# A local-attention block between two FFN layers on one core: four 64x64 tiles for the scores, values four units behind, x turned in the seventh unit

## Chip, cores and metric

The kernel runs on one core of one Trainium2 chip. The time is device microseconds of a whole execution. A comparison of this kernel can tell about 0.3% from no change.

## What is computed

The input is 4 batches of 2048 tokens of 256 numbers (float32). Three layers follow one another, each added to x:

```
x = x + 0.5 * ffn(layernorm(x));  x = x + attention(layernorm(x));  x = x + 0.5 * ffn(layernorm(x))
attention, 16 heads of 64, blocks of 128 tokens:
  q = x Wq / 8; k = x Wk; v = x Wv
  side_k, side_v: Wk, Wv on the sums of 16 tokens (128 per batch)
  logits of a block: q against the keys of the block left of it, itself, the block right of it
    (masked to |distance| <= 127 and to the batch), and against the 128 side keys
  probs = softmax with one extra logit of 0;  y = probs v;  out = y Wo
```

Only the attention phase is changed. Of the left block a query in row i sees keys i+1 and up, and of the right block keys up to i-1.

## The kernel before

**Precision.** Operands are kept as two float16 parts, high and low, and each product is three matmuls (high by high, high by low, low by high). So each stage writes a high part (ScalarE, `high`, L1263, or `split_high`, L1302) and then a low part (VectorE, `low`, L1346; for the probabilities GpSimd, `split_low`, L1013).

**Units.** The 64 blocks of 128 tokens are done in 16 rounds of `RING` = 4 blocks, and a block in 16 units, one for each head. Every engine has its program written out unit by unit, and each runs its own list in order. For head v:

- TensorE makes its scores (`scores`, L1122 and L1125) four to seven units ahead. It does four heads at once, as two pairs, in units 0, 4, 8 and 12 of a block. A pair is an even head in partitions 0 to 63 and an odd head in 64 to 127, each a matmul of 64 rows by 128 columns (a 64x128 tile) into its own PSUM bank. Key tiles whose ring slots are neighbours are one matmul.
- VectorE adds the mask and takes the maximum four units ahead (`largest`, L1354), ScalarE takes the exponential three ahead (L1286), the high parts are made two ahead (L1302, for every fourth head VectorE, L1366), then the low parts on GpSimd.
- SyncE issues one DMA transpose of both parts one unit ahead (L987), into one of `NPARTS` = 6 buffers.
- TensorE does its 12 matmuls of values `PV_LAG` = 3 units behind (`values`, L1147), so in unit u those of head u - 3. They wait for the landed transpose (`turned`).

**Items.** Between scores and values TensorE works through the projections of neighbouring blocks in pieces, as `PIECES` lists them by unit: V1 and V0, Q0, Q1, K0, K1, the output projection OUTP in four pieces, and three turns by matmuls with the identity: XTR (normalised x of a later block), YT1 and YT0 (the two halves of y). What a unit finishes, ScalarE and VectorE take out of PSUM at their next unit (`due`): ScalarE first thing in its unit, VectorE first thing in units 0, 4, 8, 12 and after `largest` in the others. XTR and YT1 use the same bank (`y_ps[1]`). XTR waits for `normalise_y` of the earlier block's second half, YT1 for XTR's low part, and OUTP's third piece (unit 10) for YT1's low part:

```
def project_out(bank, turned_y, pieces=(0, 1, 2, 3)):
    if 2 in pieces:
        pe.wait_ge(lo_done, turned_y + 1)
```

**Keys** are stored as `[slot, part, head pair, token]`, a ring of four blocks and a fifth slot with the side keys. The order of the four key tiles changes with the block's place in its round, so that slots stand next to each other where they can.

Of the kernel before, what the change touches and what calls it, by code (L numbers as in the profile page):

```python
# [6 lines left out]
F16 = mybir.dt.float16  # L7
# [8 lines left out]
P = 128  # L16
# [4 lines left out]
H, DH = 16, 64  # L21
# [13 lines left out]
FRONT, BEHIND = 1, 3  # L35
# [6 lines left out]
class Persistent:  # L42
# [24 lines left out]
    def block(self, n):  # L67

        if isinstance(n, int):
            return self.x[:, FRONT + n, :]  # L70
        return self.x[:, bass.ds(n + FRONT, 1), :].rearrange("p a d -> p (a d)")
# [626 lines left out]
def attention_phase(nc, w):  # L698
# [23 lines left out]
    V1, Q0, XTR, Q1, YT1, K0, OUTP, K1, YT0, V0 = PLAIN = range(10)  # L722
    SK0, SK1, SV0, SV1 = range(10, 14)
    FIRST_ORDER = [SK1, V1, Q0, XTR, Q1, SV1, YT1, K0, OUTP, K1, YT0, V0]
    LAST_ORDER = [V1, Q0, XTR, Q1, YT1, K0, SK0, OUTP, K1, YT0, V0, SV0]
# [5 lines left out]
    PIECES = [[(V1, 0)], [(V1, 1)], [(Q0, 0)], [(Q0, 1)], [(XTR, 0), (Q1, 0)], [(Q1, 1)], [(OUTP, 0)], [(OUTP, 1), (YT1, 0)],  # L731
              [(K0, 0)], [(K0, 1)], [(OUTP, 2)], [(OUTP, 3)], [(K1, 0)], [(K1, 1)],
              [(YT0, 0), (V0, 0)], [(V0, 1)]]
    XTR_SLOT = 4
# [12 lines left out]
    SCORE_AHEAD, EXP_AHEAD, SPLIT_AHEAD, TURN_AHEAD, PV_LAG = 4, 3, 2, 1, 3  # L747
    NBUF = 4
    NPARTS = 6
# [9 lines left out]
    with ExitStack() as ctx:  # L759
# [17 lines left out]
        kr = sb("k_parts", [P, RING + 1, 2, HD], F16)  # L777
# [45 lines left out]
        y_cleared = sem("y_cleared")  # L823
# [127 lines left out]
        def tiles_of(at, v):  # L951
# [4 lines left out]
            return tiles if place == INNER else tiles[1:]  # L956

# [90 lines left out]
        def _(pe):  # L1048
# [53 lines left out]
            def scores(at, v):  # L1102
# [9 lines left out]
                cols = slice(pair * P, (pair + 1) * P)  # L1112
                todo, started = tiles_of(at, v), False
                while todo:

                    (t, slot), n = todo[0], 1
                    while n < len(todo) and todo[n][1] == slot + n:
                        n += 1
                    todo = todo[n:]
                    for q_part, k_part in ((HI, HI), (HI, LO), (LO, HI)):  # L1120
                        ends = not todo and q_part == LO
                        even = nc.tensor.matmul(score_ps[v % NBUF][:, t * P:(t + n) * P],  # L1122
                                                qs[0:DH, j % 2, q_part, cols], kr[0:DH, slot:slot + n, k_part, cols],
                                                start=not started, stop=ends, skip_group_check=True)
# [59 lines left out]
            for index, (kind, n) in enumerate(PRE):  # L1184
                if index == FIRST_SCORES:
                    pe.wait_ge(lo_done, FIRST_SCORES)
                    for v in range(0, SCORE_AHEAD, 2):
                        scores(At(0, 0), v)
# [311 lines left out]
```

## Time and profile before

| | |
|---|---|
| median of 3 runs | 2176.99 us (2176.89 to 2182.71) |
| profiled execution, its own time | 2183.18 us |
| its span | 2181.5 us |
| attention phase in it | 310 to 1928 us, 1618 us |
| FFN phases | 0 to 310 us, 1928 to 2181 us |
| busy share of the whole span: TensorE, VectorE, ScalarE, GpSimd | 94%, 86%, 88%, 64% |
| mean granted TensorE clock, share of 2.4 GHz | 0.991 |

The busy share of an engine is the time in which at least one of its instructions runs. For TensorE matmuls (PE) and weight loads (PEld) are told apart; matmuls are pipelined, so that a matmul's duration is longer than the distance from its start to the next start. That distance is what it costs in a stream.

### The profile page before, as it was taken

Reading aid. Unit: us, or ns where it says so; the run is one execution under the profiler, and the core shown is the slowest. Engines: PE = TensorE matmul, PEld = TensorE weight load, DVE = VectorE, ACT = ScalarE, POOL = GpSimd, SP = SyncE. Lnnn points to the kernel's source line nnn. Section 1 sums busy time; section 2 is a strip of 40 time slices with the busy share of each in tenths; the row PEclk is TensorE's granted clock in tenths of the full one; section 3 lists DMA queues with packets and bytes.
Section 4 is the critical chain, followed back from the end, with each engine's and each line's share of the span. In section 5 each row is a group of like instructions: output and inputs, shape, how many; then the busy total and the mean of one; then the engine's idle time right before and its main releaser. Section 6 shows DMA issues by size and latency. Waiting matters only on the chain. (4 is left out here: it accounts for less than half of the span.)

```text
span 2181.5 us, 77479 instructions
## 1 busy us (share of the span) xinstructions
PE 2049.6 (94%) x30286; PEld 1567.5 (72%) x30286; DVE 1879.6 (86%) x4646; ACT 1930.1 (88%) x4210; POOL 1406.1 (64%) x1455
## 2 busy tenths in 40 slices
PE   5999979999999999999999999999999999979999
PEld 3666657777777777777777778777777777746666
DVE  7999968889998898898979899998889889867776
ACT  5899958999999899999989999998999999969997
POOL 2444536777787687777767777786777777722221
PEclk9999989999999999999999999999999999989999
DMA  7888837999999899999989999999999999958998
GB/s 210 154 156 153 158 61 124 172 166 176 171 173 171 132 174 170 172 178 168 171 143 162 172 174 169 178 179 152 149 171 172 169 177 175 163 87 177 179 179 182
DMA packets 1341581, 355.54 MB, mean 163 GB/s; under 512 B 1321760, under 2 KB 1340192, under 8 KB 1341216
## 3 DMA queue, kind: packets, MB, share of 16 engines
q1 hardware_dynamic: 1341216, 350.59, 100.4%
q8 instruction: 239, 3.92, 0.7%
q14 instruction: 126, 1.03, 0.2%
HBM read 14.68 MB, written 8.39 MB: 11 GB/s over the span
## 5 line engine op out<-in xcount | busy, mean ns | idle before, releaser
L1013 POOL TENSOR_TENSOR probs_split<-probs,probs_split 128x512 f16<-128x512 f32 (+1 forms) x1026 | 1159.3, 1130 | 385.3 <-ACT probs_split L1302 281.3
L1286 ACT ACTIVATE probs<-probs,minus_max 128x512 f32<-128x512 f32 (+1 forms) x1027 | 717.0, 698 | 27.1 <-DVE minus_max L1354 26.9
L1354 DVE CUSTOM_DVE_ANT_0 probs<-score_ps,mask,neg_qk_scale 128x512 f32<-128x512 f32 (+1 forms) x1028 | 723.5, 716 | 9.6 <-PE score_ps L1125 8.3
L1147 PEld LDWEIGHTS y_ps<-v_parts,probsT 128*128 128x128 f16 x11904 | 457.7, 98 | 149.4 <-DMA probsT<-probs_split 71.1
L1147 PE MATMUL y_ps<-v_parts,probsT 128*128 128x64 f16 x11904 | 514.8, 193 | 51.4 <-DMA probsT<-probs_split 49.8
L1302 ACT ACTIVATE probs_split<-probs 128x512 f16<-128x512 f32 (+1 forms) x770 | 470.2, 611 | 8.5 <-DMA probsT<-probs_split 0.3
L1122 PE MATMUL score_ps<-k_parts,q_parts 64*128 64x384 f16 (+3 forms) x2604 | 371.1, 286 | 4.7 <-DVE k_parts L1346 2.7
L1125 PE MATMUL score_ps<-k_parts,q_parts 64*128 64x384 f16 (+3 forms) x2604 | 371.1, 286 | 0.0
L1122 PEld LDWEIGHTS score_ps<-k_parts,q_parts 64*128 64x128 f16 x2604 | 200.5, 94 | 108.0 <-issue 13.2
L1054 PE MATMUL item_ps<-b_xT,wk_split 128*128 128x128 f16 x3168 | 221.7, 220 | 1.9 <-DVE v_parts L1346 1.5
L1054 PE MATMUL item_ps<-wo_split,yT_parts 128*128 128x256 f16 x1560 | 213.9, 274 | 6.1 <-DVE v_parts L1346 4.6
L1054 PE MATMUL item_ps<-b_xT,wq_split 128*128 128x128 f16 x3120 | 218.2, 220 | 1.2 <-DVE b_xT L1346 0.9
L1054 PE MATMUL item_ps<-wv_split,b_xT 128*128 128x512 f16 x786 | 212.3, 380 | 0.0
L1054 PEld LDWEIGHTS item_ps<-b_xT,wk_split 128*128 128x128 f16 x3168 | 180.3, 98 | 35.7 <-issue 22.1
L1366 DVE CAST probs_split<-probs 128x512 f16<-128x512 f32 (+1 forms) x256 | 181.0, 707 | 27.8 <-ACT probs L1286 27.7
L1125 PEld LDWEIGHTS score_ps<-k_parts,q_parts 64*128 64x128 f16 x2604 | 200.4, 94 | 0.0
L1286 ACT ACTIVATION_READ_ACCUMULATOR probs<-probs,minus_max 128x1 f32 x1027 | 194.2, 189 | 0.0
L1054 PEld LDWEIGHTS item_ps<-b_xT,wq_split 128*128 128x128 f16 x3120 | 178.6, 98 | 18.7 <-issue 12.9
L1054 PEld LDWEIGHTS item_ps<-wo_split,yT_parts 128*128 128x128 f16 x1560 | 135.7, 98 | 19.5 <-DVE v_parts L1346 5.1
L1346 DVE TENSOR_TENSOR yT_parts<-y_ps,yT_parts 128x512 f16<-128x512 f32 x129 | 88.5, 686 | 54.4 <-ACT yT_parts L1263 54.3
L1346 DVE TENSOR_TENSOR v_parts<-item_ps,v_parts 128x512 f16<-128x512 f32 x140 | 95.7, 686 | 43.5 <-ACT v_parts L1263 43.4
L1263 ACT ACTIVATE k_parts<-item_ps 128x512 f16<-128x512 f32 x141 | 84.2, 597 | 53.8 <-PE item_ps L1054 51.5
(172 smaller groups left out, 3452.1 us busy)
## 6 DMA issues: line engine op xcount, KB each, us to landing
probsT<-probs_split SPq DMA_TRANSPOSE x1025, 3.9
out_x<-x_resident SPq DMA_DIRECT2D x64, 128.0 KB, 2.0
x_resident<-in_L_attn_x SPq DMA_DIRECT2D x56, 128.0 KB, 2.7
h_a<-in_L_ffn_w_up SPq DMA_DIRECT2D x1, 1024.0 KB, 5.8
scratch_a<-in_L_ffn_w_down SPq DMA_DIRECT2D x1, 1024.0 KB, 8.0
x_resident<-in_L_attn_x SPq DMA_DIRECT2D x2, 512.0 KB, 9.4
raw_q_a<-in_L_attn_Wq SPq DMA_DIRECT2D x1, 1024.0 KB, 11.5
raw_k_a<-in_L_attn_Wk SPq DMA_DIRECT2D x1, 1024.0 KB, 11.8
```

The source lines that it names most:

```text
L1013: nc.gpsimd.tensor_tensor(parts_of[ring(at, v)][:, LO, low_columns(place_of(at, v))], probs[v % NBUF][:, cols], parts_of[ring(at, v)][:, H ...
L1054: last = nc.tensor.matmul(out, left(k, a), right(k, b), start=(k == 0 and m == 0), stop=(k == n - 1 and m == 2))
L1122: even = nc.tensor.matmul(score_ps[v % NBUF][:, t * P:(t + n) * P], qs[0:DH, j % 2, q_part, cols], kr[0:DH, slot:slot + n, k_part, cols], ...
L1125: odd = nc.tensor.matmul(score_ps[v % NBUF + 1][:, t * P:(t + n) * P], qs[DH:P, j % 2, q_part, cols], kr[DH:P, slot:slot + n, k_part, cols ...
L1147: last = nc.tensor.matmul(out, pt[ring(at, v)][:, low * a + t, :], vr[:, slot, b, h * DH:(h + 1) * DH], start=(n == 0), stop=(n == len(pas ...
L1263: nc.scalar.activation(dst, src, ACT.Copy).then_inc(hi_done, 1)
L1286: nc.scalar.activation(probs[v % NBUF][:, cols], probs[v % NBUF][:, cols], ACT.Exp, bias=bias[:, j % 2, h:h + 1], scale=-1.0, accum_out=su ...
L1302: nc.scalar.activation(parts_of[ring(at, v)][:, HI, cols], probs[v % NBUF][:, cols], ACT.Copy).then_inc(phi_done[v % 4], 1)
L1346: nc.vector.tensor_tensor(dst, src, hi, ALU.subtract).then_inc(lo_done, 1)
L1354: nc.vector.tensor_tensor_reduce(out=probs[v % NBUF][:, cols], in0=score_ps[v % NBUF][:, cols], in1=mask_of(at, v), scale=w.neg_qk_scale[: ...
L1366: nc.vector.tensor_copy(parts_of[ring(at, v)][:, HI, cols], probs[v % NBUF][:, cols]).then_inc(phi_done[v % 4], 1)
```

## The change

- `scores`: the 64x128 tiles become 64x64 tiles, four at a time: two halves of the queries (`side` 0 and 1) by two heads. The half of the right block's keys that queries 0 to 63 can't see is left out for them, and the half of the left block's keys that queries 64 to 127 can't see. A new function `key_runs` gives the runs of neighbouring keys for each side. The parts are now the outer loop, the runs the inner one.
- The keys' layout becomes `[part, head pair, slot and token]`.
- The four score banks are cleared on VectorE once at the phase's start, and TensorE waits for this once.
- `PV_LAG` 3 to 4, `NPARTS` 6 to 7. `invert_denominators` and `normalise_y` move one unit later.
- XTR moves from unit 4 (after Q1's piece) to unit 6 (before OUTP's), YT1 from unit 7 to 8. OUTP's third piece stays in unit 10.
- Two of three spare blocks behind the resident x are dropped, and `block` clips its index.

```diff
-FRONT, BEHIND = 1, 3
+FRONT, BEHIND = 1, 1
...
-    V1, Q0, XTR, Q1, YT1, K0, OUTP, K1, YT0, V0 = PLAIN = range(10)
+    V1, Q0, Q1, XTR, YT1, K0, OUTP, K1, YT0, V0 = PLAIN = range(10)
...
-    PIECES = [[(V1, 0)], [(V1, 1)], [(Q0, 0)], [(Q0, 1)], [(XTR, 0), (Q1, 0)], [(Q1, 1)], [(OUTP, 0)], [(OUTP, 1), (YT1, 0)],
-              [(K0, 0)], [(K0, 1)], [(OUTP, 2)], [(OUTP, 3)], [(K1, 0)], [(K1, 1)],
+    PIECES = [[(V1, 0)], [(V1, 1)], [(Q0, 0)], [(Q0, 1)], [(Q1, 0)], [(Q1, 1)], [(XTR, 0), (OUTP, 0)], [(OUTP, 1)],
+              [(K0, 0), (YT1, 0)], [(K0, 1)], [(OUTP, 2)], [(OUTP, 3)], [(K1, 0)], [(K1, 1)],
               [(YT0, 0), (V0, 0)], [(V0, 1)]]
-    XTR_SLOT = 4
+    XTR_SLOT = 6
...
-    SCORE_AHEAD, EXP_AHEAD, SPLIT_AHEAD, TURN_AHEAD, PV_LAG = 4, 3, 2, 1, 3
+    SCORE_AHEAD, EXP_AHEAD, SPLIT_AHEAD, TURN_AHEAD, PV_LAG = 4, 3, 2, 1, 4
     NBUF = 4
-    NPARTS = 6
+    NPARTS = 7
     CLEARED = 4
...
-        kr = sb("k_parts", [P, RING + 1, 2, HD], F16)
+        kr = sb("k_parts", [P, 2, NPAIR, (RING + 1) * P], F16)
...
+        def key_runs(at, v, side):
+
+            order, runs = order_of(at, v), []
+            for t, slot in tiles_of(at, v):
+                first = DH if order[t] == LEFT and side == 1 else 0
+                end = DH if order[t] == RIGHT and side == 0 else P
+                to, source, n = t * P + first, slot * P + first, end - first
+                if runs and runs[-1][0] + runs[-1][2] == to and runs[-1][1] + runs[-1][2] == source:
+                    runs[-1][2] += n
+                else:
+                    runs.append([to, source, n])
+            return runs
...
-                cols = slice(pair * P, (pair + 1) * P)
-                todo, started = tiles_of(at, v), False
-                while todo:
-
-                    (t, slot), n = todo[0], 1
-                    while n < len(todo) and todo[n][1] == slot + n:
-                        n += 1
-                    todo = todo[n:]
-                    for q_part, k_part in ((HI, HI), (HI, LO), (LO, HI)):
-                        ends = not todo and q_part == LO
-                        even = nc.tensor.matmul(score_ps[v % NBUF][:, t * P:(t + n) * P],
-                                                qs[0:DH, j % 2, q_part, cols], kr[0:DH, slot:slot + n, k_part, cols],
-                                                start=not started, stop=ends, skip_group_check=True)
-                        odd = nc.tensor.matmul(score_ps[v % NBUF + 1][:, t * P:(t + n) * P],
-                                               qs[DH:P, j % 2, q_part, cols], kr[DH:P, slot:slot + n, k_part, cols],
-                                               start=not started, stop=ends, skip_group_check=True)
-                        started = True
+                runs = [key_runs(at, v, side) for side in range(2)]
+                last = {}
+                for q_part, k_part in ((HI, HI), (HI, LO), (LO, HI)):
+                    for run in range(max(map(len, runs))):
+                        for side in range(2):
+                            if run >= len(runs[side]):
+                                continue
+                            queries = slice(pair * P + side * DH, pair * P + (side + 1) * DH)
+                            to, source, n = runs[side][run]
+                            ends = q_part == LO and run == len(runs[side]) - 1
+                            for odd in range(2):
+                                rows = slice(odd * DH, (odd + 1) * DH)
+                                last[odd] = nc.tensor.matmul(
+                                    score_ps[v % NBUF + odd][side * DH:(side + 1) * DH, to:to + n],
+                                    qs[rows, j % 2, q_part, queries], kr[rows, k_part, pair, source:source + n],
+                                    start=(run == 0 and q_part == k_part), stop=ends, skip_group_check=True)
+                even, odd = last[0], last[1]
...
+                    pe.wait_ge(scores_cleared, NBUF)
...
+                    if h == XTR_SLOT:
+                        block_item(at, b, j, XTR, (0,))
                     for kind, piece in PIECES[h]:
                         if kind not in TURNS:
                             block_item(at, b, j, kind, (piece,))
-                    if h == XTR_SLOT:
-                        block_item(at, b, j, XTR, (0,))
...
+            values(end, -4)
...
-                return kr[:, slot, part, 512 * c:512 * c + 512]
+                return kr[:, part, 4 * c:4 * c + 4, slot * P:(slot + 1) * P]
...
+            for n in range(NBUF):
+                nc.vector.memset(score_ps[n][:], 0.0).then_inc(scores_cleared, 1)
...
-                    if h in (2, 10):
-                        invert_denominators(at, u - 3)
                     if h in (3, 11):
-                        normalise_y(at, u - 4, at.before(j) if h == 3 else at.item(j, YT1) + 1)
+                        invert_denominators(at, u - 4)
+                    if h in (4, 12):
+                        normalise_y(at, u - 5, at.before(j) if h == 4 else at.item(j, YT1) + 1)
                     for n, kind in due_late(at, u):
```

## Rows read from the trace of the kernel before

**Rows 1.** Windows: span's phases; per engine busy us (instructions), clock, DMA share.
```profile
310.00:1928.00 1618.00, 1549.03 (x26662) 1226.64 (x26662) 1417.30 (x3505) 1465.42 (x3559) 1215.97 (x1221) 1.00 1.08 164
...
500.00:1700.00 1200.00, 1154.87 (x20011) 915.28 (x20008) 1062.36 (x2629) 1101.02 (x2679) 918.50 (x922) 1.00 1.10 167
```

**Rows 2.** Groups by form, 500 to 1700 us, VectorE: out<-in xcount | busy, mean ns | idle.
```profile
L1402 DVE RECIPROCAL inv_denominator<-denominator 128x8 f32<-128x8 f32 x97 | 18.1, 187 | 0.0
```

**Rows 3.** Waits of the attention phase: engine, for what: us, times, longest.
```profile
PEld y_ps L1147 <- DMA probsT<-probs_split: 71.1, 124, 1.7
...
ACT k_parts L1263 <- PE item_ps L1054: 51.5, 104, 2.6
...
PEld item_ps L1054 <- issue: 45.5, 144, 0.4
...
ACT yT_parts L1263 <- PE y_ps L1087: 32.2, 51, 2.4
...
ACT b_xT L1263 <- PE y_ps L1080: 16.8, 18, 6.8
...
DVE probs L1354 <- PE score_ps L1125: 8.3, 16, 1.1
...
PEld score_ps L1122 <- DVE minus_max L1354: 6.5, 27, 0.5
...
PEld item_ps L1054 <- DVE yT_parts L1346: 5.2, 10, 1.7
```

**Rows 4.** Timeline of TensorE's matmuls: start, us, line, out<-in, count [idle before].
```profile
993.18 0.83 PE L1054 MATMUL item_ps<-b_xT,wk_split 128*128 128x128 f16 x12
...
994.20 0.82 PE L1054 MATMUL item_ps<-wo_split,yT_parts 128*128 128x256 f16 x6
...
998.75 0.83 PE L1054 MATMUL item_ps<-b_xT,wk_split 128*128 128x128 f16 x12
1000.14 0.52 PE L1147 MATMUL y_ps<-v_parts,probsT 128*128 128x64 f16 x12 [0.56 <-DMA probsT<-probs_split]
```

**Rows 5.** The DMA transposes: durations of issue, and to landing.
```profile
L987 SPq DMA_TRANSPOSE probsT<-probs_split x1025: 1209/1287/2722, 327.3 to 1917.4; - x171
...
DMA to landing us min/median/max: 2.7/3.9/6.0
```

**Rows 6.** Waits of the DMA queue, 500 to 1700 us.
```profile
SPq L987 <- POOL probs_split L1013: 564.7, 621, 2.6
```

**Rows 7.** Timeline of score matmuls, one run of 512 keys.
```profile
990.75 0.39 PE L1122 MATMUL score_ps<-k_parts,q_parts 64*128 64x512 f16 x1
...
990.97 0.38 PE L1122 MATMUL score_ps<-k_parts,q_parts 64*128 64x512 f16 x1
...
991.84 0.38 PE L1122 MATMUL score_ps<-k_parts,q_parts 64*128 64x512 f16 x1
...
992.15 0.56 PE L1054 MATMUL item_ps<-b_xT,wk_split 128*128 128x128 f16 x7
```

**Rows 8.** Timeline of weight loads in a burst of scores.
```profile
1003.13 0.09 PEld L1122 LDWEIGHTS score_ps<-k_parts,q_parts 64*128 64x128 f16 x1
1003.13 0.09 PEld L1125 LDWEIGHTS score_ps<-k_parts,q_parts 64*128 64x128 f16 x1
1003.18 0.09 PEld L1122 LDWEIGHTS score_ps<-k_parts,q_parts 64*128 64x128 f16 x1
```

**Rows 9.** All engines' timeline around the turn YT0.
```profile
1001.47 0.42 PEld L1087 LDWEIGHTS y_ps<-ident,y 128*128 128x128 f32 x4
1001.50 0.64 PE L1087 MATMUL y_ps<-ident,y 128*128 128x128 f32 x4
...
1001.97 0.81 PE L1054 MATMUL item_ps<-wv_split,b_xT 128*128 128x512 f16 x3
...
1002.17 0.60 ACT L1263 ACTIVATE yT_parts<-y_ps 128x512 f16<-128x512 f32 x1 [0.66 <-PE y_ps L1087]
...
1002.80 0.69 DVE L1346 TENSOR_TENSOR yT_parts<-y_ps,yT_parts 128x512 f16<-128x512 f32 x1
```

**Rows 10.** Same view, VectorE in units 8 and 9 of a block.
```profile
993.00 0.73 DVE L1366 CAST probs_split<-probs 128x512 f16<-128x512 f32 x1
...
993.65 0.74 DVE L1354 CUSTOM_DVE_ANT_0 probs<-score_ps,mask,neg_qk_scale 128x512 f32<-128x512 f32 x1
```

**Rows 11.** Groups by line, a PSUM bank cleared by VectorE.
```profile
L1413 DVE MEMSET y_ps<- 128x512 f32 x1 | 0.5, 485 | 0.5 <-PEq L84 0.5
```

More of the change, by code:

```diff
@@ L67, in block @@
     def block(self, n):
-        if isinstance(n, int):
-            return self.x[:, FRONT + n, :]
-        return self.x[:, bass.ds(n + FRONT, 1), :].rearrange("p a d -> p (a d)")
+        return self.x[:, FRONT + min(n, NBLK), :]
 def prepare(nc, w, x_in, wq, wk, wv, wo, w_up, w_down):
@@ L698, in attention_phase @@
 def attention_phase(nc, w):
-    V1, Q0, XTR, Q1, YT1, K0, OUTP, K1, YT0, V0 = PLAIN = range(10)
+    V1, Q0, Q1, XTR, YT1, K0, OUTP, K1, YT0, V0 = PLAIN = range(10)
     SK0, SK1, SV0, SV1 = range(10, 14)
-    FIRST_ORDER = [SK1, V1, Q0, XTR, Q1, SV1, YT1, K0, OUTP, K1, YT0, V0]
-    LAST_ORDER = [V1, Q0, XTR, Q1, YT1, K0, SK0, OUTP, K1, YT0, V0, SV0]
+    FIRST_ORDER = [SK1, V1, Q0, Q1, SV1, XTR, YT1, K0, OUTP, K1, YT0, V0]
+    LAST_ORDER = [V1, Q0, Q1, XTR, YT1, K0, SK0, OUTP, K1, YT0, V0, SV0]
     BANK_OF = {V1: 0, Q0: 1, Q1: 0, K0: 0, OUTP: 1, K1: 0, V0: 1, SK1: 1, SV1: 1, SK0: 0, SV0: 0}
@@ L822, in attention_phase @@
         dve_step, cleared, half_set = sem("b_dve_step"), sem("b_cleared"), sem("half_set")
-        y_cleared = sem("y_cleared")
+        y_cleared, scores_cleared = sem("y_cleared"), sem("scores_cleared")
         block = ctx.enter_context(nc.Block())
@@ L1246, in result @@
                 return bank[:, 0:KD * P].rearrange("p (k n) -> p k n", k=KD)
-            return bank[:].rearrange("p (c n) -> p c n", c=4) if kind in (YT0, YT1) else bank[:]
+            return bank[:].rearrange("p (c n) -> p c n", c=4) if kind in (YT0, YT1, *KEYS) else bank[:]
         def ring_slot(j, kind):
```

## Prediction

> **What bounds the kernel now.** I read the phases first. The attention phase is 1618 us of the span, and all changed lines but one constant lie in it [rows 1]. In its middle 1200 us the reciprocal of the denominators, done twice a block, ran 97 times [rows 2], so a block takes 1200 / 48.5 = 24.74 us, or 1.55 us a unit. In the same window TensorE is busy 1154.9 us, ScalarE 1101.0 and VectorE 1062.4 [rows 1], which is 23.8, 22.7 and 21.9 us of a block. Three engines are thus nearly full, and TensorE is first. The table of waits tells what the rest is. TensorE's weight loads for the values waited for the landed transpose 71.1 us in 124 places, 0.57 us each and 1.7 us at most; that is the largest wait TensorE has. Other waits of TensorE are small: 6.5 us for VectorE's maxima before scores, 5.2 us for YT's low part before the output projection [rows 3]. ScalarE in turn waited for TensorE's items: 51.5 us for keys, 32.2 for turned y, 16.8 for turned x [rows 3]. So each of the two is sometimes ahead of the other, and both waits come from too little room between them. VectorE nearly never waits for scores (8.3 us) [rows 3].
>
> The timeline shows one such stall. A piece of 12 matmuls starts at 998.75. Two such pieces elsewhere stand 1.02 us apart with the values (12 matmuls, about 0.35 us) between them, so the piece itself streams for 0.67 us and ends at 999.42. The values start at 1000.14 [rows 4]: 0.72 us lost. The transposes are not at their limit: an issue lasts 1.29 us (median), 16 of them 20.6 us of a block of 24.74 [rows 5], and in 1200 us their queue waited 564.7 us for GpSimd's low parts [rows 6]. Landing takes 3.9 us (median, 2.7 to 6.0) [rows 5].
>
> **The scores.** Before, a pair with one run of 512 keys makes three passes, 0.217 us apart (990.75 to 990.97), and two pairs take 990.75 to 992.06, with 0.09 us more until the next item starts [rows 7]. An odd and an even matmul run side by side, so a pass costs its 512 columns: 0.213 us. After, each side of an inner block streams 448 keys a pass. If the four tiles run side by side, each at its own pace, a pass costs 448 columns: 0.187 us. The saving is 0.0267 x 3 passes x 8 pairs = 0.64 us a block. The first and last blocks of a batch give nothing: one of their two sides still streams all 384 keys. So 56 blocks x 0.64 = 36 us, all on TensorE.
>
> This rests on two things that no row shows. First, the sides' runs differ in length (320 and 128 against one of 448; 64 and 384 against 128 and 320). If each run had to wait for the longer of its partners, the passes of a round would be 512, 448, 576 and 512 columns, 512 in the mean, and the saving nil. Second, the weight loads: 8 a pass (6 where one side has one run) instead of 4 or 2, each of 64 columns. In a 128-key run of before, two loads and two matmuls pass every 0.05 to 0.06 us, and both loads start at the same time, while the matmuls before them still stream [rows 8]. That is at most 0.028 us a load even if they took turns; 8 such loads are 0.224 us a pass. The slowest loads in the trace are those of the float32 turns: four loads of 128 columns with their matmuls pass in 0.47 us (1001.50 to 1001.97) [rows 9], at most 0.118 us each, 0.059 for half the columns. Eight in turn would be 0.47 us a pass, two at a time 0.236. The bounds are therefore -36 us (hidden) and +395 us ((0.47 - 0.213) x 24 passes x 64 blocks). I take hidden, as the nearest row, a load with 64 rows, shows loads that start together beside running matmuls.
>
> The Trainium skill speaks against this edit: "TensorEngine Tiling (Array Packing)", Gotcha 2, says that column tiling excludes fast weight load. By the page "TensorE: Matmul & The Clock Gate", LDWEIGHTS, a load is its columns over 1.2 GHz, 53 ns for 64, and eight in turn would be 427 ns, an estimate that would add (0.427 - 0.213) x 1536 = 328 us. The same page's Part 3 says that a load overlaps running matmuls only in another row group; rows 8 differ: the load for a tile starts while its own rows still stream.
>
> **Values one unit later.** A value's transpose gets one more unit. TensorE's short units are 1.02 us apart [rows 4], so waits below that vanish, and the mean is 0.57. The buffers grow with it (7 for 6), so the transposes start no later: SyncE waits for the values of v - 7, which TensorE does in the same unit as v - 6 before. Below, the bound is no gain (if ScalarE's chain sets the pace, the wait returns); above, 71 us. With the other terms a block comes to 23.9 us against ScalarE's 22.7 busy, so ScalarE will now and then be late; I keep about a quarter: -55 us. VectorE's `normalise_y` is one unit later, as is the pass that it waits for. XTR in unit 6 then has two units of room, and YT0 in unit 14 still more than one.
>
> **YT1 in unit 8: a new wait.** OUTP's third piece stays in unit 10 and needs YT1's low part. From YT1's end to it TensorE now has only the second piece of K0 and the values: 1.02 us (993.18 to 994.20) [rows 4]; before, all of unit 8 with its burst of scores lay between as well. The turn YT0 shows the chain: the next item starts at 1001.97, ScalarE's high part at 1002.17, and VectorE's low part ends at 1003.49 (1002.80 + 0.69) [rows 9], 1.52 us. So TensorE stops for 0.50 us a block, 32 us in 64. VectorE has this item behind its cast and its maximum in unit 9. In the block shown these start at 993.00 and end at 994.39 [rows 10], and the low part of 0.69 us would end at 995.08, 0.88 us after 994.20: 56 us. Where TensorE would have waited anyway, it costs nothing. I take 0.50: without YT1 in unit 8's VectorE list, that engine gets to unit 9 0.69 us sooner. XTR in unit 6 needs no such term: K0 comes after a burst of scores, whose second pair, over 0.65 us long, itself waits for VectorE's unit 7.
>
> **The rest.** Four clears of PSUM at 0.485 us [rows 11] are 1.9 us, beside the first turn and its copies: +1. The keys' stores write four chunks of 128, as many elements as before: 0. The extra values at the end replace those of the loop: 0. Some 5,950 more matmuls are in the first term. Spare blocks: 0.
>
> **Sum:** -36 - 55 + 32 + 1 = -58 us. The profiled execution took 2183.2 us, so 2125; it was 6 us above the median of the runs, so 2119. I forecast 2120, its own range 2090 to 2150 (yT wait 0 to 56, transposes' wait 35 to 71 gone, and ScalarE's own waits a little less).
>
> **Rivals.**
> - Loads bound the scores (the other side). Tiles of 64 columns load one after the other. The terms without the scores are -55 + 32 + 1 = -22 us; over 1536 passes that is 14 ns. So from 0.227 us a pass, 28 ns a load, the kernel is slower. Two at a time at the float32 rate (0.236) give 2155 + 35 = 2190, all in turn about 2550. For it: twice as many loads, none of this shape in the trace. Against it: rows 8. Chance 0.18.
> - The tiles bring nothing: runs wait for their longer partner. 2120 + 36 = 2156. Against it: even and odd tiles run side by side today, but always with equal lengths. Chance 0.17.
> - ScalarE sets the pace and the lag buys little: of the transposes' wait 20 us go, and the new wait stands. -36 - 20 + 32 + 1 = -23, 2154. For it: ScalarE's 22.7 of 24.74 us. Against it: ScalarE itself waits for items. Chance 0.13; within 0.3% if YT1's wait is 0.88 us (2178).
> - The forecast: chance 0.52.
>
> Slower by over 0.3%: the loads' 0.18 and 0.03 of the third. Within 0.3%, which is about what a measurement can tell from no change: 0.07, from the two middle rivals with the dearer wait. Faster: 0.72. The range 2090 to 2200 takes in the middle rivals and the milder half of the first.
>
> **What would show it.** Starts of one pass to the next in a 512-key burst: 0.187 us right, 0.21 or more wrong. The transposes' wait near 16 us. Item matmuls of the output projection waiting for yT's low part: some 32 us, against 5.2. ScalarE's waits for keys and turned x smaller, its busy share up from 92% to about 95%. I would be wrong if loads of 64 columns show gaps between the score matmuls, or if the granted clock fell below the 1.00 of the phase.

## The result: slower, and the profile after

The change made the kernel slower. After it took 2210.80 us (median of 4, 2206.58 to 2213.70), before 2179.85 (median of 4, 2176.89 to 2183.10, run beside it): a ratio of 1.0142, 95% interval 1.0122 to 1.0162. The prediction was 2120 with a range of 2090 to 2200: it had the sign wrong, and the time lies outside the range. The profiled execution took 2213.7 us, a span of 2212.0.

The phase of the attention, which was 1618 us [rows 1], is now 1645. These are the windows of the kernel after, with the columns of [rows 1], and then TensorE's groups for values and scores on its page:

```profile
310.00:1955.00 1645.00, 1536.43 (x32614) 1286.43 (x32614) 1409.79 (x3507) 1462.14 (x3559) 1211.93 (x1221) 1.00 1.11 161
500.00:1700.00 1200.00, 1127.27 (x24067) 944.96 (x24066) 1038.24 (x2580) 1078.17 (x2629) 897.38 (x903) 1.00 1.13 164
```
```profile
L1158 PEld LDWEIGHTS y_ps<-v_parts,probsT 128*128 128x128 f16 x11904 | 454.8, 98 | 158.5 <-DMA probsT<-probs_split 100.2
...
L1135 PE MATMUL score_ps<-k_parts,q_parts 64*64 64x128 f16 (+6 forms) x11184 | 345.7, 265 | 7.0 <-DVE k_parts L1359 2.7
L1135 PEld LDWEIGHTS score_ps<-k_parts,q_parts 64*64 64x64 f16 x11184 | 255.7, 107 | 47.2 <-DVE minus_max L1367 10.2
```

In the same 1200 us every engine is busy for less than before: TensorE 1127 for 1155 us, ScalarE 1078 for 1101, VectorE 1038 for 1062. A block now takes 25.21 us (mean over the blocks but the first, between turns of x) and took 24.71. So none of these engines got more to do per unit of work, they all wait more. TensorE's clock is 1.00 of its full speed in both. What rose is the DMA share, from 1.08 to 1.11 of sixteen engines in the phase and from 1.10 to 1.13 in its middle.

**The scores did become shorter.** The timeline of TensorE's matmuls in one block of after (start, us, line, tiles, count):

```profile
1001.82 1.39 PE L1135 MATMUL score_ps<-k_parts,q_parts 64*64 64x320 f16 x36
1003.14 0.84 PE L1065 MATMUL item_ps<-b_xT,wk_split 128*128 128x128 f16 x12
1003.82 0.51 PE L1158 MATMUL y_ps<-v_parts,probsT 128*128 128x64 f16 x12
1004.17 0.64 PE L1098 MATMUL y_ps<-ident,y 128*128 128x128 f32 x4
1004.64 0.83 PE L1065 MATMUL item_ps<-b_xT,wk_split 128*128 128x128 f16 x12
1005.31 0.51 PE L1158 MATMUL y_ps<-v_parts,probsT 128*128 128x64 f16 x12
1006.37 0.83 PE L1065 MATMUL item_ps<-wo_split,yT_parts 128*128 128x256 f16 x6 [0.54 <-DVE yT_parts L1359]
...
1008.37 0.52 PE L1158 MATMUL y_ps<-v_parts,probsT 128*128 128x64 f16 x12 [0.17 <-DMA probsT<-probs_split]
1008.82 1.35 PE L1135 MATMUL score_ps<-k_parts,q_parts 64*64 64x64 f16 x48
1010.10 0.84 PE L1065 MATMUL item_ps<-b_xT,wk_split 128*128 128x128 f16 x12
```

The burst of two pairs at 1008.82 has 48 matmuls and the next item starts 1.28 us after it; in [rows 7] it was 12 matmuls and 1.40 us. Over all 257 bursts of the trace, from the first score matmul's start to the next item's, the median fell from 1.416 to 1.277 us and the sum from 355 to 331 us. The loads of 64x64 are hidden, and a pass costs the columns of its side, not those of the longer run: with 448 columns a side the passes start 0.19 us apart, against 0.22 us for 512 in [rows 7]. At 1006.37 stands the wait for y's low part that the prediction had expected of YT1's new place.

**What is waited for.** The table of waits over the phase, as in [rows 3]:

```profile
PEld y_ps L1158 <- DMA probsT<-probs_split: 100.2, 159, 1.9
ACT yT_parts L1276 <- PE y_ps L1098: 97.7, 78, 3.2
...
DVE probs L1367 <- PE score_ps L1135: 62.9, 104, 1.4
...
PEld item_ps L1065 <- DVE yT_parts L1359: 42.0, 98, 1.7
...
ACT k_parts L1276 <- PE item_ps L1065: 28.0, 44, 2.6
```

The wait for the landed transpose, which was to shrink from 71.1 to some 16 us, rose to 100.2. The wait for y's low part is 42.0 us against 5.2. ScalarE's and VectorE's waits for TensorE rose too (yT 97.7 against 32.2, scores 62.9 against 8.3), as they do when TensorE comes late. Added up from these, in us: scores -24, transposes +29, YT1's low part +37, TensorE's idle time before loads of items that no wait explains (`issue`) -9 (45.5 to 36.3), together +33; the profiled executions differ by 30.5.

**What else changed** stands in a part of the page that the prediction never opened, the DMA queues. First the middle 1200 us of before, then of the first experiment (the tiles alone), packets, MB and share:

```profile
q1 hardware_dynamic: 794573, 197.15, 109.3%
q8 instruction: 158, 2.59, 0.9%
q14 instruction: 77, 0.63, 0.2%
```
```profile
q1 hardware_dynamic: 777053, 192.80, 111.9%
q8 instruction: 189, 3.10, 1.1%
q14 instruction: 74, 0.61, 0.2%
```

Queue 1 holds the transposes. Queue 8 brings TensorE its code: over the whole kernel 286 packets of 16 KB after and 239 before. The scores are 11,184 matmuls and were 5,208, so TensorE got 5,976 more and as many loads: 47 x 16,384 bytes over 11,952 instructions are 64 bytes each. They look like nothing (0.7% of the engines' time, now 0.9%). What one does is seen in a small window. This is the DMA view of after, 1313 to 1317.6 us, in 40 slices of 0.115 us, and the timeline of TensorE in the same stretch:

```profile
DMA  9999998799999999995799999900000000005999
GB/s 209 225 220 194 180 201 163 147 200 229 214 203 216 200 198 214 185 174 94 158 207 352 223 169 76 33 0 0 0 2 7 9 9 9 11 9 98 280 285 287
...
q8 instruction: 1, 0.02, 1.3%
```
```profile
1315.41 0.81 PE L1065 MATMUL item_ps<-wv_split,b_xT 128*128 128x512 f16 x3
1317.54 0.52 PE L1158 MATMUL y_ps<-v_parts,probsT 128*128 128x64 f16 x12 [1.32 <-DMA probsT<-probs_split]
```

The one fetch starts at 1315.49 (the slice with 352 GB/s). From 1315.99 to 1317.14 all sixteen engines move next to nothing, although SyncE is in the midst of an issue; then the transposes go on, one lands at 1317.49, and the values, which had stood for 1.32 us, start at 1317.54. Over the phase, from the records of the landings and of the packets (a packet counted where its middle lies): two transposes land 1.15 us apart (mean) in before if no packet of code lies between, and 2.87 us apart if a fetch of queue 8 does (185 intervals); in after 1.10 and 2.85 us (228). A fetch thus holds up a landing by 1.7 us. There are 209 of them between the first and the last landing in before, 255 in after.

**Who pays for it.** The engine that never rests is SyncE. Its own records show it, in a view that the tables of busy engines leave out (least, median and greatest ns of an issue, after):

```profile
L998 SPq DMA_TRANSPOSE probsT<-probs_split x1025: 1209/1287/2736, 327.6 to 1950.6; - x171
```

The median issue lasts 1.29 us, but the mean is 1.43 in before and 1.47 in after. In before the 1025 issues of the phase last 1468.7 us in sum, and 0.09 us (median) pass from the end of one to the start of the next: some 1564 us out of the 1592 from the first start to the last end. Each low part had been ready for 1.4 us (median) when SyncE took it up, and SyncE really waited for one only 24 us in all. What makes the mean longer than the median is the fetches: 190 issues of before take over 1.6 us (2.06 in the mean), and for 98% of them a fetch starts during the issue or at most 0.5 us ahead of it, against 12% of the others. In the window above the issue from 1315.44 takes 2.11 us. In after the sum of the issues is 1506.5 us, 38 more for 46 more fetches, and the span grew by 30.5. These are sums that fit; that the fetches are the cause, and not a companion, is for the experiments to show.

### The profile page after: what moved, and what is told of

Its sections match the earlier page's. It is cut to its first block and busy times, and to the rows that moved or that the text cites. A ratio compares the mean times of both kernels' runs of the same rounds, so it can differ in the third digit from the quotient of the medians.

```text
span 2212.0 us, 89436 instructions
## 1 busy us (share of the span) xinstructions
PE 2039.3 (92%) x36262; PEld 1629.4 (74%) x36262; DVE 1873.0 (85%) x4650; ACT 1926.9 (87%) x4210; POOL 1402.1 (63%) x1455
## 5 line engine op out<-in xcount | busy, mean ns | idle before, releaser
L1367 DVE CUSTOM_DVE_ANT_0 probs<-score_ps,mask,neg_qk_scale 128x512 f32<-128x512 f32 (+1 forms) x1028 | 731.1, 724 | 63.3 <-PE score_ps L1135 62.9
L1158 PEld LDWEIGHTS y_ps<-v_parts,probsT 128*128 128x128 f16 x11904 | 454.8, 98 | 158.5 <-DMA probsT<-probs_split 100.2
L1135 PE MATMUL score_ps<-k_parts,q_parts 64*64 64x128 f16 (+6 forms) x11184 | 345.7, 265 | 7.0 <-DVE k_parts L1359 2.7
L1135 PEld LDWEIGHTS score_ps<-k_parts,q_parts 64*64 64x64 f16 x11184 | 255.7, 107 | 47.2 <-DVE minus_max L1367 10.2
L1379 DVE CAST probs_split<-probs 128x512 f16<-128x512 f32 (+1 forms) x256 | 172.2, 673 | 18.0 <-ACT probs L1299 9.2
L1276 ACT ACTIVATE yT_parts<-y_ps 128x512 f16<-128x512 f32 x129 | 77.0, 597 | 98.1 <-PE y_ps L1098 97.7
L1359 DVE TENSOR_TENSOR q_parts<-item_ps,q_parts 128x512 f16<-128x512 f32 x130 | 89.5, 689 | 75.4 <-ACT q_parts L1276 75.4
L353 DVE TENSOR_TENSOR h_split_c<-h_c,h_split_c 128x1024 f16<-128x1024 f32 x64 | 78.4, 1225 | 58.3 <-ACT h_split_c L658 57.1
L280 POOL TENSOR_TENSOR h_rms_c<-mean_square_c,pow_exp_c 128x4 f32<-128x4 f32 x16 | 16.5, 1030 | 165.1 <-ACT scratch_c L662 165.1
```

The source lines that it names most:

```text
L353: nc.vector.tensor_tensor(h_parts[LO][n % RING_H], h[n % 2], h_parts[HI][n % RING_H], ALU.subtract).then_inc(hlo_ready, 1)
L1135: last[odd] = nc.tensor.matmul(score_ps[v % NBUF + odd][side * DH:(side + 1) * DH, to:to + n], qs[rows, j % 2, q_part, queries], kr[rows, ...
L1158: last = nc.tensor.matmul(out, pt[ring(at, v)][:, low * a + t, :], vr[:, slot, b, h * DH:(h + 1) * DH], start=(n == 0), stop=(n == len(pas ...
L1359: nc.vector.tensor_tensor(dst, src, hi, ALU.subtract).then_inc(lo_done, 1)
L1367: nc.vector.tensor_tensor_reduce(out=probs[v % NBUF][:, cols], in0=score_ps[v % NBUF][:, cols], in1=mask_of(at, v), scale=w.neg_qk_scale[: ...
L1379: nc.vector.tensor_copy(parts_of[ring(at, v)][:, HI, cols], probs[v % NBUF][:, cols]).then_inc(phi_done[v % 4], 1)
```

## The experiments

Each ratio is that of the kernel's time to runs of the kernel before that stood beside it on the same chip. "Wait for transposes" is the row `PEld y_ps <- DMA` in 310:1960.

**1. One part at a time.** Four kernels. The first has the tiles (with the keys' layout, the clears and the spare blocks) in the schedule of before, `PV_LAG` 3 and 6 buffers; the second only the order of XTR and YT1; the third order, lag and buffers, with the scores of before; the fourth everything, with XTR in unit 5 behind Q1's second piece and YT1 back in unit 7. All kernels of the experiments have the change's smaller number of spare blocks; e2_lag_order below, within 0.3% of before, shows that this costs nothing that can be measured.

```diff
# e1_tiles, against after
-    SCORE_AHEAD, EXP_AHEAD, SPLIT_AHEAD, TURN_AHEAD, PV_LAG = 4, 3, 2, 1, 4
+    SCORE_AHEAD, EXP_AHEAD, SPLIT_AHEAD, TURN_AHEAD, PV_LAG = 4, 3, 2, 1, 3
-    NPARTS = 7
+    NPARTS = 6
# and PIECES, FIRST_ORDER, LAST_ORDER, XTR_SLOT as before
# e4_mid, against after
-... [(Q1, 1)], [(XTR, 0), (OUTP, 0)], [(OUTP, 1)], [(K0, 0), (YT1, 0)], ...
+... [(Q1, 1), (XTR, 0)], [(OUTP, 0)], [(OUTP, 1), (YT1, 0)], [(K0, 0)], ...
-    XTR_SLOT = 6
+    XTR_SLOT = 5
```

> The 64x64 tiles alone, with the schedule of before (values three units behind, six buffers, XTR in unit 4, YT1 in unit 7). Theory A (the tiles save TensorE time, as the bursts of the changed kernel show, and the loss comes from where XTR and YT1 now stand): bursts of scores as short as in the changed kernel and a time some 15 to 30 us below before, 2150 to 2165. Theory C (the tiles themselves cost more elsewhere than they save, for instance because VectorE gets its first scores later: it waited 62.9 us for scores in the changed kernel, 8.3 before): no faster than before, VectorE's wait for scores at 30 us or more.

Measured: 2218.40 us, 1.0158 (1.0133 to 1.0182). The tiles alone cost all of it and a little more. The wait for transposes is the largest on TensorE:

```profile
PEld y_ps L1158 <- DMA probsT<-probs_split: 135.3, 210, 2.0
```

Its bursts of scores sum to 327 us, 28 less than before: the tiles save on TensorE and lose more than that outside it.

> Only the new places of XTR (unit 6) and YT1 (unit 8), with 64x128 tiles, values three units behind and six buffers. Theory A: the whole loss is here, some 35 to 60 us above before (2215 to 2240), with TensorE's wait for yT near 0.5 us a block and ScalarE's wait for the turned y near 98 us. Theory B (the later values and the seventh buffer cost the time, the places do not): within 10 us of before, though with a wait for yT.

Measured: 2191.52 us, 1.0035 (1.0015 to 1.0054). Item matmuls wait 55.2 us for y's low part in this run, and the wait for transposes falls to 27.2: a wait of 50 us came, one of 44 went, and the time rose by 8. That is within 10 us of before, but not for the reason expected with it, as the next run shows.

> The changed kernel without the tiles: values four units behind, seven buffers, new places of XTR and YT1. Theory A: 2230 to 2245, the changed kernel plus the 25 to 36 us that the tiles save. If the lag removes waits for the transposes as I had forecast, it is 30 us or more below the run with the new places alone. Theory C: at or below the changed kernel, 2200 to 2212.

Measured: 2185.79 us, 1.0009 (0.9995 to 1.0023). The wait for transposes falls to 13.4 us, as the prediction had it for the lag (16), and the kernel is no faster. Both times expected of this run, 2230 to 2245 and 2200 to 2212, were missed.

> The changed kernel with XTR in unit 5 (behind Q1's second piece) and YT1 back in unit 7; tiles, lag of four and seven buffers stay. Theory A: the round trip at YT1 is gone, TensorE's wait for yT falls to under 10 us, ScalarE's for the turned y to 40 or less, and the time is 2125 to 2150. Theory B: it stays at 2190 or more.

Measured: 2215.58 us, 1.0154 (1.0128 to 1.0181). The wait for y's low part is gone (4.4 us), the wait for transposes is 123.4. So neither the places nor the lag explain the loss; the tiles do, in every schedule. Waits of TensorE move from row to row at nearly the same time of the kernel: none of them is the bound.

**2. Is it the tile or the instruction?** The 64x128 tiles of before, but every run of keys cut in two: the same columns, about 5,200 matmuls and loads more, no 64x64 tile. Only the keys' layout and the spare blocks are those of the change.

```diff
# f4_cut, against before (in scores)
                     for q_part, k_part in ((HI, HI), (HI, LO), (LO, HI)):
-                        even = nc.tensor.matmul(score_ps[v % NBUF][:, t * P:(t + n) * P], ...
+                        for m in range(2):
+                            out = slice(t * P + m * half_run, t * P + (m + 1) * half_run)
+                            even = nc.tensor.matmul(score_ps[v % NBUF][:, out], ...
```

> The 64x128 tiles and the schedule of before, keys in the new layout, but every run of keys cut into two matmuls: 5,200 more matmuls and weight loads for the same columns. Theory D (TensorE's instructions are fetched by the DMA engines that also carry the transposes; more instructions are more fetches, and each delays a transpose): slower by 20 to 45 us, with the values' wait for the transposes at 110 us or more, as with the 64x64 tiles. Theory T (it is something of the 64x64 tile itself): within 10 us of before, that wait near 71 us.

Measured: 2208.25 us, 1.0102 (1.0072 to 1.0131). 280 packets of TensorE's code against 239, bursts of scores 360 us against 355, the wait for transposes 94.6:

```profile
q8 instruction: 280, 4.59, 0.9%
```
```profile
PEld y_ps L1162 <- DMA probsT<-probs_split: 94.6, 164, 1.6
```

Instructions without any tile cost 20 us, four times what they add to the bursts. (The wait was expected at 110 us or more.)

**3. Are the transposes the bound?** Less and more to turn, and less for TensorE. In the first two kernels only the high parts of the probabilities are turned, half the elements (and the values use them twice). The third turns a ninth tile of 128 columns that nobody reads. The fourth leaves out the third of the three passes of the projections of Q and K.

```diff
# f1_half (f2_tiles_half is the same edit on e1_tiles)
-            return split if place_of(at, v) == INNER else split[:, P:7 * P]
+            return split[:, 0:4 * P] if place_of(at, v) == INNER else split[:, P:4 * P]
# f3_nine
-            return split if place_of(at, v) == INNER else split[:, P:7 * P]
+            return split[:] if place_of(at, v) == INNER else split[:, P:8 * P]   # nine tiles
# g8_lean (projections of Q and K)
+                                         range(KD), KD, ((HI, HI), (HI, LO)))
```

> Before with half of every transpose left out: only the high parts of the probabilities are turned, and the low passes of the values read the high tiles. All instructions of TensorE stay. Theory D: with the DMA engines half empty the values' wait falls from 71 us to under 20, and the time by 20 to 60 us. If the chain of ScalarE and GpSimd sets the pace, the time falls by less than 15 us.

Measured: 2135.86 us, 0.9768 (0.9743 to 0.9793), wait for transposes 26.8 us (expected under 20). SyncE's view, and the middle 1200 us:

```profile
L998 SPq DMA_TRANSPOSE probsT<-probs_split x1025: 1177/1217/2775, 326.2 to 1872.2; - x171
```
```profile
500.00:1700.00 1200.00, 1178.05 (x20588) 943.09 (x20585) 1084.48 (x2701) 1127.09 (x2751) 944.82 (x947) 1.00 0.54 87
```

The DMA share fell by half, from 1.10 to 0.54, and the median issue only from 1.29 to 1.22 us. The issues in sum are 44 us shorter, the time 52.

> Before with a ninth tile in every transpose (one eighth more to turn, nobody reads it). Theory D, in its strong form (the busiest DMA engine is full: transposes 20.5 us a block and some 3.3 fetches of about 1.2 us): 80 to 150 us slower. If the transposes have the room that their queue's idle time shows: less than 30 us slower.

Measured: 2274.10 us, 1.0406 (1.0373 to 1.0438), wait for transposes 138.1 us. An eighth more to turn costs 86 us, though no computing engine got any work in its loop. The median issue is 1.38 us long, and the issues in sum are 82 us longer.

> Before with the third pass (low part of the first operand by high part of the second) of the query and key projections left out: 2048 matmuls of 128 columns less, 115 us of TensorE's stream at 0.056 us each. If TensorE bounds the kernel, as I had read it: 80 us or more faster. Theory D: only the 16 fetches less count, at about 1.7 us each in which the transposes' landings are stretched: 10 to 35 us faster, and the values' wait for the transposes grows above 100 us.

Measured: 2161.77 us, 0.9901 (0.9874 to 0.9927). 2,048 matmuls fewer leave TensorE 1096.46 us busy in the middle 1200 and the wait for transposes at 140.3:

```profile
500.00:1700.00 1200.00, 1096.46 (x18681) 835.01 (x18678) 1066.83 (x2666) 1109.75 (x2716) 930.90 (x935) 1.00 1.11 169
```
```profile
PEld y_ps L1158 <- DMA probsT<-probs_split: 140.3, 178, 2.0
```

From TensorE's stream 115 us went (2,048 x 0.056), from the time 23. TensorE does not set the pace of the kernel before. (222 packets of code against 239: with 17 fewer fetches SyncE's issues are 13 us shorter in sum, so over half of the 23 need not be TensorE's; this was not tried apart.)

> The same halved transposes under the tiles-alone kernel. Theory D: the loss by the tiles is gone and their saving shows: 10 to 25 us below the kernel with halved transposes and 64x128 tiles. Theory T: 15 us or more above it, as with full transposes (35 us).

Measured: 2163.89 us, 0.9896 (0.9870 to 0.9921), wait for transposes 80.6 us. Here an expectation failed: with half the elements to turn, the tiles still cost 28 us against their twin, nearly as much as with all of them. The records say why: what a fetch does to an issue doesn't shrink with the transpose. With the tiles the issues of the halved kernels last 1452.0 us in sum, without them 1424.7, and these 27 us are the 28 that the tiles cost. The DMA engines are half empty in both (share 0.56 and 0.54), so it is not their total load that counts. A fetch still holds up what it meets: in f2_tiles_half a transpose takes 2.48 us (median) from issue to landing if no fetch starts in between and 3.83 if one does.

**4. The longer lag under full and under halved transposes.** All with lag 4, 7 buffers and the order of e4_mid: full with 64x128 tiles, halved with 64x64, halved with 64x128.

```diff
# g7_lag_mid = e4_mid with scores() and the keys' layout of before
# g5_tiles_lag_half = e4_mid with the halved transposes of f1_half
# g6_lag_half = g7_lag_mid with them
```

> Whole transposes, 64x128 tiles, values four units behind, seven buffers, XTR in unit 5 and YT1 in unit 7. Theory D: the queue of the transposes sets the pace, so more lead buys nothing: 2170 to 2190, within 10 us of before. Theory A (room between TensorE and the chain was missing, and YT1 in unit 8 ate what the lag gave): 2140 or less.

Measured: 2178.50 us, 0.9975 (0.9960 to 0.9991). The lag, the buffers and places without a new wait are worth some 6 us of the 55 that the prediction gave them, though they cut the wait for transposes only to 56.8 us. It is the fastest kernel here that leaves nothing out, by less than 0.3%.

> The twin with 64x128 tiles: halved transposes, values four units behind, seven buffers, XTR in unit 5, YT1 in unit 7. Theory D: 2120 to 2140, little or nothing below the kernel with halved transposes alone (2136), as that had only 27 us of waits left.

Measured: 2147.46 us, 0.9835 (0.9808 to 0.9862), with no wait for transposes worth a row. That is above the 2120 to 2140 expected, and above f1_half's 0.9768: here the longer lag made the kernel slower. SyncE's issues sum to the same (1423.1 us), but it waits 42 us for low parts where it waited 26 in f1_half.

> Halved transposes (low parts not turned), 64x64 tiles, values four units behind, seven buffers, XTR in unit 5 and YT1 in unit 7. Theory D (a fetch of TensorE's code holds up the transposes; the tiles' shorter bursts count only where the transposes have room in rate and in lead): below its twin with 64x128 tiles by 10 us or more, so 2100 to 2125, with a values' wait under 25 us. Theory T (the 64x64 tile costs elsewhere): above its twin by 15 us or more.

Measured: 2164.07 us, 0.9907 (0.9880 to 0.9934), wait for transposes 43.4 us. Missed too: where only a third of the issues end before the transpose ahead has landed (36%, and 28% in the twin, against 98% in before), the tiles should have begun to pay, and they cost 17 us. SyncE's issues are 24 us longer in sum than the twin's.

**5. The instruction again, and TensorE with room to spare.** The cut of f4_cut in the last two schedules, and the tiles in the kernel with the leaner projections.

```diff
# h1_cut_lag_half = g6_lag_half with the cut of f4_cut
# h2_cut_lag      = g7_lag_mid with the cut of f4_cut
# h3_lean_tiles   = e1_tiles with the projections of g8_lean
```

> The kernel with halved transposes (high parts of the probabilities only; the low parts are not turned and the values use the high ones twice), values four units behind and seven buffers, that took 0.9835 of the kernel before. Here each of its score runs of 128 keys and more is cut in two, so TensorE gets about 5,200 more matmuls and as many loads for the same columns and no 64x64 tile. Theory of the instructions (what costs is the fetching of TensorE's code, on the DMA engines and into TensorE): as slow as the kernel with tiles, which took 0.9907, so 0.990 (0.987 to 0.994), 2163. Rival (the 64x64 tiles cost by themselves when transposes are cheap): the twin's 0.9835 plus at most the 5 us that the cut added to the bursts of scores elsewhere, 0.984 to 0.986, 2150.

Measured: 2163.14 us, 0.9916 (0.9893 to 0.9939), that of the kernel with tiles. Instructions alone explain the residue that run g5_tiles_lag_half had left.

> Nothing left out. The same cut of the score runs, with full transposes, values four units behind, seven buffers, x turned in the fifth unit and y in the seventh; its uncut twin took 0.9975 of the kernel before, the same schedule with tiles 1.0154. Theory of the instructions: the cut costs what it cost in the schedule of before (0.0102) or more, so 1.008 to 1.015, about 2207. Rival (the fetches delay the values only by moments, which a lead of one more unit covers): 0.998 to 1.003, 2185.

Measured: 2210.96 us, 1.0124 (1.0103 to 1.0145); 1.5% over its twin. The wait for transposes rose from 56.8 to 89.9 us. A unit more of lead does not cover the fetches, since what they take is SyncE's time, not a moment's delay of one landing.

> The third pass (low part of x by high part of the weights) of the projections of Q and K is left out, as in the run that took 115 us of work from TensorE and only 23 us from the time (0.9901), and the scores go by four 64x64 tiles in the schedule of before. Theory of the queue (the transposes and the fetches bound both kernels, and TensorE has over 100 us to spare): the tiles cost here what they cost with full work, 0.013 to 0.017, so 1.003 to 1.007, about 2195. Rival (the tiles cost TensorE's own time): with 115 us of slack the cost shrinks below 0.005, so at most 0.995, 2172.

Measured: 2193.93 us, 1.0054 (1.0028 to 1.0081); against g8_lean's 0.9901 the tiles cost 1.5%, as much as with full work:

```profile
PEld y_ps L1158 <- DMA probsT<-probs_split: 210.8, 260, 2.5
```

With 115 us less to stream, TensorE absorbs none of it. The wait for transposes, 140.3 us in g8_lean, grows by 70: the 32 us lost and the streaming that the tiles save both end up there.

**6. What all runs have in common.** One number from each trace, with the span of the same execution: the sum of SyncE's issues of the phase's 1025 transposes. Differences are to before (sum 1468.7 us, span 2181.5).

| run | fetches in the phase | sum of the issues | difference | difference of the span |
|---|---|---|---|---|
| after | 255 | 1506.5 | +38 | +31 |
| e1_tiles | 255 | 1508.7 | +40 | +37 |
| e3_order | 209 | 1469.2 | +1 | +3 |
| e2_lag_order | 209 | 1469.6 | +1 | +3 |
| e4_mid | 255 | 1507.2 | +39 | +32 |
| f4_cut | 249 | 1501.8 | +33 | +30 |
| f1_half | 209 | 1424.7 | -44 | -46 |
| f2_tiles_half | 255 | 1452.0 | -17 | -20 |
| f3_nine | 209 | 1551.0 | +82 | +84 |
| g5_tiles_lag_half | 255 | 1447.2 | -22 | -24 |
| g6_lag_half | 209 | 1423.1 | -46 | -36 |
| g7_lag_mid | 209 | 1470.2 | +2 | -4 |
| g8_lean | 192 | 1455.6 | -13 | -20 |
| h1_cut_lag_half | 249 | 1452.6 | -16 | -21 |
| h2_cut_lag | 249 | 1499.0 | +30 | +27 |
| h3_lean_tiles | 238 | 1490.4 | +22 | +10 |

The span follows the sum within 12 us in all of them, and within 8 in all but g6_lag_half and h3_lean_tiles. The rest is mainly in the steps between issues: 124 us in before, 134 in g6_lag_half, 112 in h3_lean_tiles, 115 to 128 in the others; 95 of these are the 0.09 us of each step, so in no run does SyncE stand still for more than some 40 us. Per fetch, the issues last 0.7 us more than the median would make them (0.8 with halved transposes, 0.65 in f3_nine). That is less than the 1.7 us of the landings, because the next landing mostly follows a held-up one by 0.9 us.

## Why the prediction was wrong, step by step

**The step that failed** is in its first part: "The transposes are not at their limit", from an issue of 1.29 us, "16 of them 20.6 us of a block of 24.74", and a queue that "waited 564.7 us for GpSimd's low parts". The median issue has no fetch in it (the longest in [rows 5] is 2.7 us) and no step to the next. With the mean of 1.43 us and the 0.09 us between two issues, 16 of them are 24.4 us of a block: SyncE is full, and it sets the pace. The 564.7 us of [rows 6] were misread. The view measures from the start of an issue to a semaphore's update during it, and SyncE is so late that this is the update for a later transpose; each issue's own low part was ready before the issue started, and the true wait is 24 us. [Rows 5] also had a sign of it: landing takes 3.9 us in the median and 2.7 at best. TensorE was "nearly full" because it stands in one ring with SyncE (values free a buffer, the buffer is split anew, turned, and waited for), not because it sets the pace. Halving what is turned took 52 us off, 115 us less of TensorE's took 23.

**The scores, -36 us.** The mechanism was right, both disputed points of it: four tiles side by side each at their own pace, loads hidden. Its size was 24 us in after and 28 in e1_tiles, as a burst of two pairs shrinks by 0.14 us where 0.16 were forecast. The rule of the Trainium skill that column tiling has no fast weight load ("TensorEngine Tiling (Array Packing)", Gotcha 2) does not show in the time, nor do the +328 us that the prediction estimated for eight loads in turn: a load of 64x64 lasts 107 ns against 98 for 128x128, but four start within 0.01 us of one another and run beside the matmuls. But the same term swallowed what decided the case, in one sentence: "Some 5,950 more matmuls are in the first term." On TensorE they are. Their code is not: it was priced at nothing, and 46 more fetches in the phase made SyncE's issues 38 us longer in sum; the stretch from the first landing to the last grew by 32 (1590.7 to 1623.0). f4_cut, h1_cut_lag_half and h2_cut_lag show the cost with no tile in the kernel.

**Values one unit later, -55 us.** Wrong in size and in reading. Where lag and buffers come without a new wait they are worth 6 us (g7_lag_mid), and nothing with the order of the change (e2_lag_order), though there the wait itself fell to 13.4 us as forecast. A wait of the engine that isn't the bound can be removed without its time. ScalarE's lateness, which the prediction weighed against it, was not the reason: SyncE's sum of issues stayed the same (1469.6 and 1470.2 us against 1468.7).

**YT1 in unit 8, +32 us.** Right as a wait: 42.0 us in 98 places, against 5.2 in 10, 0.57 us a block where 0.50 was forecast. Wrong as a price: with the order alone the kernel lost 8 us (e3_order), and with YT1 back in its place and everything else changed nothing was won (1.0154 against 1.0142).

**XTR, clears, spare blocks:** nothing is to be seen of them in the time, as forecast. XTR in unit 6 waits 5.5 us for VectorE's `normalise_y`, which empties its bank; one place earlier, in e4_mid, it waits 25.7.

**The rivals.** "Loads bound the scores" gave a time near the measured one (2190 in its milder half) for a reason that isn't there. "The tiles bring nothing" and "ScalarE sets the pace" were both milder than what came. The case that came, SyncE's transposes as the bound and TensorE's code as a load on them, was on no list; the chance of 0.21 for slower stood on another mechanism.

**What stays open.** Why a 16 KB fetch, whose packet takes 1.0 to 1.2 us (median) on its own engine, leaves all sixteen idle for as long and lengthens the issue that it meets: the records show that it does, not how. What an issue's 1.29 us are made of: half the elements shorten it by 0.07 us, an eighth more lengthen it by 0.09. Why halved transposes bring GpSimd's low parts later when the lag is longer (g6_lag_half). Fewer instructions with full transposes and all of TensorE's work, for instance tiles merged into fewer matmuls, was not tried.

## What to carry to other kernels

Read the engine that issues the DMAs as one more engine before calling TensorE the bound: add up its issues and the gaps between them, not the median issue times their count, and check a wait that a table gives it against the order of the records. The DMA share would not have told it: it was 0.54 to 0.56 in the kernels with halved transposes, where more instructions still cost 16 to 28 us. Price an edit in instructions too: where the engine that issues transposes is full, 256 more TensorE instructions (128 matmuls with their loads) cost one fetch, here 0.7 us of that engine's time, and in sum more than the columns that finer tiles save. A wait is worth its time only on the engine that is the bound; one that vanishes from one row and returns in another says to look elsewhere.

## What the runs showed of the hardware

- Code is fetched by the same DMA engines that carry the transposes. TensorE's comes in packets of 16 KB (256 instructions of 64 bytes), one each 6.4 us after and 7.6 us before; of the 135 us that TensorE stands for transposes in e1_tiles, 101 are in stalls that end 2 to 3 us after the start of such a packet, and only 16% of the phase's time lies so behind one.
- A fetch holds the whole transpose up, though it is one packet: landings 2.8 to 3.0 us apart instead of 1.0 to 1.2, in all seventeen traces. The 8 KB packets of queue 14 cost less (landings 1.6 to 1.9 us apart).
- A fetch also lengthens the issue on SyncE that it meets: 2.06 us in the mean for the issues over 1.6 us in before, against a median of 1.29.
- An issue of a transpose lasts 1.22 us (median) for half of the elements, 1.29 for all and 1.38 for an eighth more (f1_half, before, f3_nine), with 0.09 us to the next.
- Four 64x64 tiles with runs of unequal length run independently: a pass costs the columns of the longer side in sum (448 columns a side, 0.19 us from pass to pass), and eight loads of 64 columns a pass stay hidden (107 ns each, four at once).
